# The sparse-expert stage: bias matmuls over 128 rows, a wait per expert, weights fetched a stage earlier, answers fetched at once

## What is computed

```python
mla_out = ao @ o_w + o_b                      # latent attention, 16 heads
probs = softmax(mla_out @ router_w + router_b)    # 8 experts
topw, topi = top_k(probs, 2); topw /= topw.sum(-1) + 1e-8
h1 = gelu(mla_out @ w1[e] + b1[e])            # 256 -> 512, for each expert e
h2 = h1 @ w2[e] + b2[e]                       # 512 -> 256
x = layernorm(x + (x + 0.3 * sum_e combine[e] * h2))
```

## Time and profile before

| | |
|---|---|
| median of 3 runs | 3590.7 us (3590.26 to 3591.96) |
| the profiled execution: own time, span | 3593.07 us, 3590.8 us |
| granted TensorE clock over the span | 0.931 |
| PE, DVE, ACT, POOL busy | 84%, 56%, 38%, 26% |
| expert stage, opening | 3120.8 to 3181.9 us |
| slots | 3181.9 to 3515 us |
| closing | 3518.4 to 3590.8 us |

### The profile page before, as it was taken

How to read it: one execution, slowest core, us unless ns; L and a number is a source line. 1 busy time by engine, 2 the same in 40 slices (tenths; PEclk the granted TensorE clock), 3 DMA queues, 4 the chain that set the end, 5 groups by cost and what they waited for, 6 DMA issues and landing times. The chain is left out here.

```text
span 3590.8 us, 62854 instructions
## 1 busy us (share of the span) xinstructions
PE 3031.4 (84%) x17666; PEld 2116.8 (59%) x17667; DVE 2019.2 (56%) x3902; ACT 1349.6 (38%) x2815; POOL 941.3 (26%) x1262
## 2 busy tenths in 40 slices
PE   5989898998989985877999999969888888359991
PEld 4665666656666655765777777744444444247771
DVE  3656555465646556764666666556666666333334
ACT  3545445354545441222222222215444444233330
POOL 3332332333333311213333333310111111212224
PEclk8999999999999997997999999979999999679995
DMA  1000000000000002111000000022222222241115
GB/s 46 1 14 1 14 1 14 6 9 14 1 13 1 7 8 73 38 64 58 12 12 12 12 12 12 6 56 59 59 59 59 59 60 57 69 139 58 57 54 171
DMA packets 103470, 132.37 MB, mean 37 GB/s; under 512 B 16472, under 2 KB 80088, under 8 KB 102624
## 3 DMA queue, kind: packets, MB, share of 16 engines
q1 hardware_dynamic: 96352, 110.89, 10.4%
q0 software_dynamic: 6912, 18.96, 1.4%
HBM read 64.66 MB, written 36.78 MB: 28 GB/s over the span
## 5 line engine op out<-in xcount | busy, mean ns | idle before, releaser
L612 ACT ACTIVATE soft_probs<-soft_ps_s,soft_mx 128x512 f32<-128x512 f32 x512 | 348.5, 688 | 359.3 <-DVE soft_mx L516 342.6
L1328 DVE TENSOR_REDUCE mla_mx<-mla_ps_s 128x1 f32<-128x512 f32 x512 | 333.7, 685 | 198.0 <-PE mla_ps_s L1188 195.5
L1430 ACT ACTIVATE mla_pt<-mla_ps_t 128x512 f32<-128x512 f32 x512 | 290.9, 600 | 354.7 <-PE mla_ps_t L1200 349.0
L516 DVE TENSOR_REDUCE soft_mx<-soft_ps_s 128x1 f32<-128x512 f32 x512 | 328.3, 684 | 134.0 <-PE soft_ps_s L405 116.2
L416 PEld LDWEIGHTS soft_ps_p<-ident,soft_probs 128*128 128x128 f32 x2048 | 227.5, 143 | 259.2 <-ACT soft_probs L612 57.5
L416 PE MATMUL soft_ps_p<-ident,soft_probs 128*128 128x128 f32 x2048 | 316.7, 286 | 29.7 <-DVE soft_pt L536 23.1
L405 PE MATMUL soft_ps_s<-soft_ks,soft_qs 128*128 128x512 f32 x1024 | 304.9, 422 | 43.0 <-ACT soft_probs L612 32.2
L434 PE MATMUL soft_ps_m<-soft_pt,soft_v 128*64 128x512 f32 x1024 | 268.3, 610 | 1.3 <-DVE soft_v L505 1.3
L1188 PE MATMUL mla_ps_s<-mla_stack,mla_pad 128*128 128x512 f32 x512 | 229.4, 455 | 26.1 <-DVE mla_mx L1328 21.3
L536 DVE COPY soft_pt<-soft_ps_p 128x512 f32<-128x512 f32 x256 | 174.3, 681 | 104.7 <-PE soft_ps_p L416 103.9
L1200 PE MATMUL mla_ps_t<-mla_shifted,mla_pad 128*128 128x512 f32 x512 | 219.2, 430 | 14.1 <-ACT mla_pt L1430 11.7
(11 more groups left out here) (328 smaller groups left out, 6744.7 us busy)
## 6 DMA issues: line engine op xcount, KB each, us to landing
mla_pad<-mla_stack SPq DMA_DIRECT2D x256, 64.0 KB, 2.0
moe_xt<-by_expert SPq DMA_DIRECT2D x72, 129.0 KB, 2.1
mla_stack<-mla_yh SPq DMA_DIRECT2D x128, 64.0 KB, 2.1
moe_raw<-in_L_ffn_w SPq DMA_DIRECT2D x16, 512.0 KB, 5.1
moe_w1h<-answers SPq DMA_DIRECT2D x16, 512.0 KB, 6.2
soft_xc<-in_L_attn_x SPq DMA_DIRECT2D x8, 512.0 KB, 3.9
x<-soft_r SPq DMA_DIRECT2D x32, 128.0 KB, 2.0
ffn_xc<-x SPq DMA_DIRECT2D x8, 512.0 KB, 3.9
```

The lines of the kernel that those rows point to most:

```text
L516: op = vv.tensor_reduce(out=mx[:, h, t:t + 1], in_=ps_s[:, t, :], axis=AX.X, op=ALU.max, negate=True)
L612: op = nc.scalar.activation(probs[:, h % 2, t, :], ps_s[:, t, :], ACT.Exp, bias=mx[:, h, t:t + 1], scale=1.0, accum_out=rs[:, h, t:t + 1])
L1328: op = vv.tensor_reduce(out=mx[:, a, t, s:s + 1], in_=ps_s[:, (16 * a + 4 * t + s) % S_BANKS, :], axis=AX.X, op=ALU.max, negate=True)
L1430: op = nc.scalar.activation(pt[:, t, s, :], ps_t[:, s % 2, :], ACT.Exp, scale=KPH ** -0.5)
```

## The change

- Latent attention: its SP queue issues the first four weight pieces between `ones_ready` and `spread`. `pt` has two buffers in place of four, and the exponent waits for the product two tiles back.
- Opening: pieces 4 to 7 are fetched as before, then come the blank rows, two DMAs of the bias parts to DRAM, pieces 8 to 11, one DMA that brings the bias parts back to two partitions, pieces 12 to 15, and the tiles.
- `bias` and `ones` span 128 partitions; rows 2 to 127 are zero (POOL and DVE clear them).
- TensorE's one wait for all low parts is gone. For each tile, the sequencer reads a second number from the table, 2e+2, and waits for so many low parts. The table takes 16 steps.
- Closing: all fetches of `answers` and of `x` go out in a row, with cells for all eight batches. ACT normalises, with a scale and a shift, and stores from its own queue. POOL makes the shift with two more operations.

```diff
-        pt = sb("pt", [P, TT, 4, SEQ])
+        pt = sb("pt", [P, 2, 4, SEQ])
...
                 hold(sp, ones_ready, 2)
+                for dst, src, done in pieces_in:
+                    sp.dma_start(dst, src).then_inc(done, 16)
...
                             if s == 0:
-                                act.wait_ge(*(pe_s.at(j, "A", a - 1, t) if a else pe_s.at(shift(j, -1), "A", QUADS - 1, t)))
-                            op = nc.scalar.activation(pt[:, t, s, :], ps_t[:, s % 2, :], ACT.Exp, scale=KPH ** -0.5)
+                                u = 4 * a + t - 2
+                                act.wait_ge(*pe_s.at(j if u >= 0 else shift(j, -1), "A", u % 16 // 4, u % 4))
+                            op = nc.scalar.activation(pt[:, t % 2, s, :], ps_t[:, s % 2, :], ACT.Exp, scale=KPH ** -0.5)
...
+RAW = 4
+PIECES = [(e, n) for e in range(E_) for n in range(2)]
+
+
+def piece_load(w, raw, e, n):
+
+    src = w[("w1", "w2")[n]][e].rearrange("(k p) n -> p k n", p=P)
+    return raw[:, (2 * e + n) % RAW, :].rearrange("p (k n) -> p k n", n=src.shape[2]), src
...
-        bias = sb("bias", [2, E_, F + D], F32R)
-        ones = sb("ones", [2, P], F32R)
+        bias = sb("bias", [P, E_, F + D], F32R)
+        ones = sb("ones", [P, P], F32R)
...
-        x_part = lambda b: raw[:, b % RAW, :]
-        y_part = lambda b, c: w1h[:, 2 * (b % 4) + c, :, :].rearrange("p k n -> p (k n)").bitcast(F32)
-        TABLE = 14
+        cells = lambda x, e: x[:, e, :, :].rearrange("p k n -> p (k n)").bitcast(F32)
+        x_part = lambda b: raw[:, b, :] if b < RAW else cells(w2h, b - RAW)
+        y_part = lambda b, c: cells((w1h, w1l)[c], b)
...
-                for c, (e, n) in enumerate(pieces):
-                    if c >= RAW:
-                        hold(sp, lo_split, c - RAW + 1)
-                    src = (w1, w2)[n][e].rearrange("(k p) n -> p k n", p=P)
-                    sp.dma_start(piece(e, n)[0].rearrange("p (k n) -> p k n", n=src.shape[2]), src).then_inc(staged[c % RAW], 16)
-                hold(sp, bias_split, 2)
-                for e in range(E_):
-                    for r, part in enumerate((hi_b, lo_b)):
-                        sp.dma_start(bias[r:r + 1, e, :].bitcast(F32), part[e:e + 1, :].bitcast(F32)).then_inc(bias_in, 16)
+                def stage(c):
+                    e, n = pieces[c]
+                    hold(sp, lo_split, c - RAW + 1)
+                    sp.dma_start(*piece_load(w, raw, e, n)).then_inc(staged[c % RAW], 16)
+
+                for c in range(RAW, RAW + 4):
+                    stage(c)
                 hold(sp, small_in, 16 * 6)
                 sp.dma_start(by_expert[E_ * ROOM:E_ * ROOM + E_ * P, :].rearrange("(e p) n -> p e n", p=P), w["blank"][1].bitcast(F32)).then_inc(bias_in, 16)
+                hold(sp, bias_split, 2)
+                for r, part in enumerate((hi_b, lo_b)):
+                    sp.dma_start(bias_parts[r], part.bitcast(F32)).then_inc(parts_out, 16)
+                for c in range(RAW + 4, len(pieces)):
+                    stage(c)
+                    if c == RAW + 7:
+                        hold(sp, parts_out, 32)
+                        hold(sp, cleared, 1)
+                        sp.dma_start(bias[0:2, :, :].bitcast(F32), bias_parts).then_inc(bias_in, 16)
                 hold(sp, tails_in, 16 * E_)
                 hold(sp, table_step, TABLE)
-                hold(sp, bias_in, 16 * (2 * E_ + 1))
+                hold(sp, bias_in, 32)
...
-                    if b >= 4:
-                        hold(sp, stored[b % 4], 16 * (b // 4))
                     for c in range(2):
                         at = (c * BATCH + b) * SEQ
-                        sp.dma_start(y_part(b, c).rearrange("p (t d) -> p t d", d=D), answers[at:at + SEQ, :].rearrange(tok, p=P)).then_inc(tile_in[b % 4], 16)
-                    if b >= RAW:
-                        hold(sp, summed, b - RAW + 1)
-                        sp.dma_start(x_part(b).rearrange("p (t d) -> p t d", d=D), x_in[b].rearrange(tok, p=P)).then_inc(staged[b % RAW], 16)
-                    if b >= 2:
-                        hold(sp, normed, TT * (b - 1))
-                        sp.dma_start(x_out[b - 2].rearrange(tok, p=P), y_part(b - 2, 0).rearrange("p (t d) -> p t d", d=D)).then_inc(stored[(b - 2) % 4], 16)
-                for b in (BATCH - 2, BATCH - 1):
-                    hold(sp, normed, TT * (b + 1))
-                    sp.dma_start(x_out[b].rearrange(tok, p=P), y_part(b, 0).rearrange("p (t d) -> p t d", d=D)).then_inc(stored[b % 4], 16)
-                for k in range(4):
-                    hold(sp, stored[k], 16 * (BATCH // 4))
+                        sp.dma_start(y_part(b, c).rearrange("p (t d) -> p t d", d=D), answers[at:at + SEQ, :].rearrange(tok, p=P)).then_inc(tile_in[b], 16)
+                    if b >= 1 and b + RAW - 1 < BATCH:
+                        x = b + RAW - 1
+                        sp.dma_start(x_part(x).rearrange("p (t d) -> p t d", d=D), x_in[x].rearrange(tok, p=P)).then_inc(staged[x % RAW], 16)
+                hold(sp, stored, 16 * BATCH)
...
-                pe.wait_ge(lo_split, len(pieces))
-                pe.wait_ge(bias_in, 16 * 2 * E_)
+                pe.wait_ge(bias_in, 32)
...
                         e = expert_of(i, n)
+                        split = pe.value_load(table[0:1, 2, bass.ds(U * i + n, 1)], min_val=2, max_val=2 * E_)
+                        pe.wait_ge(lo_split, split)
                         pe.wait_ge(xl_done, count(i, n) + 1)
...
-                nc.vector.memset(ones[:, :].bitcast(F32), 1.0).then_inc(made, 1)
+                nc.vector.memset(ones[:, :].bitcast(F32), 0.0).then_inc(made, 1)
+                dve.wait_ge(made, 2)
+                nc.vector.memset(ones[0:2, :].bitcast(F32), 1.0).then_inc(made, 1)
...
-                    lambda: vv.tensor_scalar(table[:, 1, :], expert[:, :], float(E_ - 1), None, ALU.min),
+                    lambda: vv.tensor_scalar(expert[:, :], expert[:, :], float(E_ - 1), None, ALU.min),
+                    lambda: vv.tensor_copy(table[:, 1, :], expert[:, :]),
+                    lambda: vv.tensor_scalar(table[:, 2, :], expert[:, :], 2.0, 2.0, ALU.mult, ALU.add),
...
-                def normalise(b):
-                    dve.wait_ge(rstd_done, b + 1)
-                    for t in range(TT):
-                        vv.tensor_scalar(y_part(b, 0)[:, D * t:D * t + D], y_part(b, 1)[:, D * t:D * t + D], mv[:, b % 2, t, 0:1], rstd[:, b % 2, t, :],
-                                         ALU.subtract, ALU.mult).then_inc(normed, 1)
-
                 for b in range(BATCH):
-                    dve.wait_ge(staged[b % RAW], 16 * (len(pieces) // RAW) + 16 * (b // RAW) + 16)
+                    x = b % RAW
+                    dve.wait_ge(staged[x], 16 * (len(pieces) // RAW) + 16 * (b // RAW) + 16)
                     dve.wait_ge(added, b + 1)
                     vv.scalar_tensor_tensor(out=y_part(b, 1), in0=x_part(b), scalar=2.0, in1=y_part(b, 0), op0=ALU.mult, op1=ALU.add).then_inc(summed, 1)
                     dve.wait_ge(summed, b + 1)
                     for t in range(TT):
                         vv.bn_stats(st6[:, b % 2, t, :], y_part(b, 1)[:, D * t:D * t + D]).then_inc(stats, 1)
-                    if b >= 1:
-                        normalise(b - 1)
+                    if b >= 2:
+                        dve.wait_ge(normed, TT * (b - 1))
                     for t in range(TT):
                         hold(dve, stats, TT * b + t + 1)
                         vv.bn_aggr(mv[:, b % 2, t, :], st6[:, b % 2, t, :]).then_inc(means, 1)
-                normalise(BATCH - 1)
...
                 slots(act, one_slot)
 
+                for b in range(BATCH):
+                    act.wait_ge(rstd_done, b + 1)
+                    for t in range(TT):
+                        nc.scalar.activation(y_part(b, 0)[:, D * t:D * t + D], y_part(b, 1)[:, D * t:D * t + D], ACT.Identity,
+                                             bias=shift_by[:, b % 2, t, :], scale=rstd[:, b % 2, t, :]).then_inc(normed, 1)
+                    act.wait_ge(normed, TT * (b + 1))
+                    nc.scalar.dma_start(x_out[b].rearrange("(t p) d -> p t d", p=P), y_part(b, 0).rearrange("p (t d) -> p t d", d=D)).then_inc(stored, 16)
...
+                nc.gpsimd.memset(bias[:, :, :].bitcast(F32), 0.0).then_inc(cleared, 1)
...
-                    hold(pool, eps_done, b + 1)
-                    nc.gpsimd.tensor_tensor(rstd[:, b % 2, :, :], vare[:, b % 2, :, :], const["minus_half"][:, :].unsqueeze(1).broadcast_to([P, TT, 1]), ALU.pow).then_inc(rstd_done, 1)
+                    hold(pool, eps_done, 3 * b + 1)
+                    nc.gpsimd.tensor_tensor(rstd[:, b % 2, :, :], vare[:, b % 2, :, :], const["minus_half"][:, :].unsqueeze(1).broadcast_to([P, TT, 1]), ALU.pow).then_inc(eps_done, 1)
+                    hold(pool, eps_done, 3 * b + 2)
```

(25 more changed lines are left out.)

13 lines of the change are left out of this document (6 added, 7 removed).

## The result

The changed kernel takes 3559.08 us (median of 4 runs, 3556.76 to 3559.84); the kernel before, run again beside it, 3591.33. The ratio is 0.9904 (95% interval 0.9887 to 0.9922), so about 32 us less. The forecast was 3552, in a range of 3536 to 3575. The profiled execution has a span of 3556.5 us against 3590.8, 34.3 less.

The account below looks back on a forecast made before the run. TensorE bounds the slots, DVE and transfers the opening, and DVE, POOL and transfers by turns the closing. From 3590.7 us, slots -10, opening -12.5 and closing -16 gave 3552 us, range 3536 to 3575.

Parts of the forecast that it names:

- Slots: Expert stage's slots: the sequencer, at 4.50 us in the loop, sets the pace; -10 us, 4.8 of it outside the loop.
- the slot of the loop: Slots in the loop: 4.60 us falls to 4.50, 56 times, a gain of 5.6 us.
- The price of a read: TensorE's sequencer: one more table read adds 0.75 us to 3.75 us of its own work per loop slot.
- rivals 2 and 3: Slots: first product's reads long, slot 4.85 us, 3575 (12%); or a 0.6 us wait stays, slot 5.3, 3610 (6%).
- the estimate of 5.4 us: Loop's slot if each register load cost the skill's 600 ns floor: 5.4 us, slower than before; the trace's 302 ns was preferred.
- Rival 1: Slots: reads are hidden and the array sets the pace at 3.82 us, 53 us gained, 3509 us; chance 6%.
- The array's gaps: TensorE's slots: 0.78 of 4.60 us hang on bias matmuls of 2 rows among 128; without them 3.82 us.
- Opening: Expert stage's start: bias transfers and blank rows no longer lie open, first product near 3169.3 against 3181.9, -12.5 us.
- the first four pieces are in place: Opening: early-fetched weights bring no sooner start, since DVE stands behind the table until its first low part.
- That each tile waits for its own expert's parts only brings nothing: Opening: waits per expert gain 0, since ACT and DVE still do all 16 pieces before preparing tiles.
- Latent stage: Stage ahead of the experts: early fetch of 2 MB and smaller `pt` cost 0; up to 6.5 us without the idle gap.
- Closing: Expert stage's end: fetches all queued, POOL sets the pace at 5.4 us a batch, -16 us.

Follow-up runs that it names:

- e1: Changed kernel without the second table read per slot, TensorE waiting once for all 16 pieces; ratio to the kernel before 0.9773.
- e2: Kernel before, with only the bias and the vector of ones over 128 rows, no new read; ratio to the kernel before 0.9858.
- e4: Changed kernel with the new register read made twice in each slot; ratio to the kernel before 1.0035.
- e3: Kernel before, with only the new table row and the new read and wait per slot, bias matmuls of 2 rows; ratio 1.0000.
- b1: Changed kernel with one wait for all pieces, first four low parts ahead of the table, next four between its steps; ratio to the kernel before 0.9735.
- e5: Changed kernel with DVE making the first four low parts ahead of the table of tiles; ratio to the kernel before 0.9885.
- e8: Changed kernel with the first four pieces fetched when the expert stage starts, not in the latent stage; ratio to the kernel before 0.9909.
- e7b: Changed kernel, but each fetch of a batch's answers waits until the batch four back is stored; ratio to the kernel before 0.9920.
- e6: Changed kernel with normalising back on DVE and without POOL's two small shift operations; ratio to the kernel before 0.9930.

## Why the prediction was right, and where its terms were off

**Slots: mechanism right, gain 7.2 in place of 10 us.** "The sequencer sets the pace, and TensorE waits some 0.7 us in each slot" holds: "issue" ahead of each first product, slots of the loop away from its end of 4.44 to 4.68 us, 4.52 on average, where 4.50 was forecast, and e1, e2 and e4 move by what that says. The term that failed is the slot of the loop, "56 x (4.60 - 4.50) = 5.6 us": it was 56 x (4.603 - 4.578) = 1.4. It left out the loop's end. The branch and what stands with it take some 0.5 us of the sequencer, once in 8 slots; before, the array's slack covered them (4.605 on average, boundary included), and now they lie open (4.97 us; 0.5 / 8 = 0.06 a slot). That is 3 of the 4.2 us; the rest is 4.52 in place of 4.50. In e3, where the array needs 4.60 us, the end of the loop shows too (4.84 to 5.09 us), in b1 not at all (3.83). Outside the loop and at its two ends the gain was 5.8 us where 4.8 was forecast, with slots of 4.13 to 4.37 us.

**The price of a read** was taken as 0.75 us from the earlier trace rows. e4 gives 0.65 in the loop for one more. For the first one b1 gives at least 4.52 - 3.83 = 0.69, so the sequencer's slot without it is 3.83 us at most, where 3.75 was taken. The load is 300 ns, and 314 at most, in all 72 new reads, and of the 144 others one is over 312: rivals 2 and 3 (slots of 4.85 and 5.3 us) have fallen. So has the estimate of 5.4 us by the 600 ns that the Trainium skill (DMA: Bandwidth & Descriptors, Latency and other measured facts) states for a `tensor_load`; the trace does not agree with that figure. Rival 1 (3.82 us) failed in the changed kernel for the reason given, and is what e1 and b1 show once the read is gone.

**The array's gaps.** The 0.78 us a slot were right: e2's loop runs at 3.88 us, b1's at 3.83, against 4.60. The rule of the Trainium skill (TensorEngine Tiling (Array Packing), Key Properties) that a change of tiling mode drains TensorE agrees with that; that a matmul of 2 rows among those of 128 is such a change is inferred, and what e2 shows is the 0.73 us of its loop.

**Opening: right (11.9 us, 12.5 forecast).** The reason holds too: the 16.7 us that lay open are down to 0.6, and DVE's last low part pays 4.1 us for it. That "the first four pieces are in place" is of no use to DVE is right for the weights (e5) and misses 1.5 us on the small tables, about 1 at the first product (e8). "That each tile waits for its own expert's parts only brings nothing" misses about 1 us as well. In e1 the single wait stands ahead of the transposes of the first tile too, from the timelines of DVE and PE:

```profile
3207.11 1.23 DVE L1751 TENSOR_TENSOR moe_w2l<-raw,moe_w2h 128x1024 fp32r<-128x1024 f32 x1 [0.22 <-ACT moe_w2h L1792]
...
3208.59 1.09 PE L1671 MATMUL moe_ps_x<-ident,moe_xt 128*128 128x128 f32 x4 [48.26 <-DVE moe_w2l L1751]
3210.26 0.79 PE L1680 MATMUL moe_ps_h<-moe_bias,moe_ones 128*128 x1 [0.59 <-DVE moe_xl L1757]
```

The first product comes 1.9 us behind the end of the last low part, against 0.6 in the changed kernel, where the transposes have run by then; the opening is 51.1 us, and 50.1 on the same chip in e4 with the waits per expert. So the opening's sum is close in part by luck: it has 1 to 2 us of gain at nothing and is 0.6 us too large all the same.

**Latent stage: right.** Of the 1.02 us by which the expert stage starts later, 0.98 were there when the latent stage began, and from there to the expert stage both take 754.2 us, so the early fetch and the smaller `pt` cost 0.

**Closing: right (16.1 us, 16 forecast, a turn of 5.36 us, 5.4 forecast),** but partly by luck in the reasoning: the fetches at once are worth 4.7 us (e7b), and taking the normalising off DVE, which the forecast priced only as ACT's 1.6 us at the end, another 4.9 (e6); ACT takes 2.07 us for it, where 1.6 was forecast. Without it POOL's turn would have been longer, not shorter. The other 6.5 us of the 16.1 were not taken apart: they are what the two bring only together, or what the other edits of the closing bring.

The median lies 7 us above the forecast: 2.8 from the slots, 0.6 from the opening, 1.0 from ahead of the changed code, 2.0 because the medians differ by 32.3 us where the profiled spans differ by 34.3, and 0.6 because the kernel before came out that much higher beside it.

## What to carry to other kernels

TensorE has two paces here, that of its array and that of the sequencer that feeds it, and a busy share of 100% tells only of the slower one: before making the array faster, add up the sequencer's instructions of one turn, register reads at 0.65 to 0.75 us and the loop's branch included. A wait on a value from memory costs that much even when the wait itself is long met; where a constant does, as here, it gives 44 us for one line (e1; the first product comes about 1 us later for it). And what is fetched earlier helps only if the engine that uses it is not standing behind something else: look for its first use, not for its landing.
